# Gated cross-attention block: raw input transposed early, its scale in the rotary table, one GELU pass with a GpSimd copy

## The reference

```
xn  = rmsnorm(layernorm(x)) * (1 + rms_scale)          # per token
q   = rope(xn @ q_w) / 8 ;  k = rope(rmsnorm(mem) @ k_w) ;  v = rmsnorm(mem) @ v_w
x   = x + tanh(g_xattn) * (softmax(mask(q k^T)) v) @ out_w
h   = gelu(layernorm(x) @ ternary(W1)^T + b1)          # 256 -> 1024
x   = x + tanh(g_ffn) * (h @ ternary(W2)^T + b2)       # 1024 -> 256
```

## Time and profile before

| what | value |
|---|---|
| device time, median of 3 runs | 352.86 us (352.55 to 353.22) |
| profiled execution | span 350.0 us from first to last instruction; around it some 2.9 us to the median |
| PE / PEld busy | 313.3 us (90%) / 288.6 us (82%) |
| DVE busy | 276.2 us (79%) |
| ACT busy | 235.6 us (67%) |
| POOL busy | 129.7 us (37%) |
| TensorE clock, mean over the span | 0.961 |
| chain that ended last | PE 42%, DVE 18%, issue 18%, POOL 12%, ACT 6%, DMA 2% |

### The profile page before, as it was taken

How to read it: one execution, slowest core, us unless ns; L and a number is a source line. 1 busy time by engine, 2 the same in 40 slices (tenths; PEclk the granted TensorE clock), 3 DMA queues, 4 the chain that set the end, 5 groups by cost and what they waited for, 6 DMA issues and landing times.

```text
span 350.0 us, 6845 instructions
## 1 busy us (share of the span) xinstructions
PE 313.3 (90%) x2171; PEld 288.6 (82%) x2171; DVE 276.2 (79%) x855; ACT 235.6 (67%) x595; POOL 129.7 (37%) x151
## 2 busy tenths in 40 slices
...
DMA packets 12982, 13.35 MB, mean 38 GB/s; under 512 B 1780, under 2 KB 12396, under 8 KB 12956
## 3 DMA queue, kind: packets, MB, share of 16 engines
...
q0 software_dynamic: 128, 0.21, 0.7%
...
## 4 chain that ended last, share of the span: by engine, by line
PE 42%; DVE 18%; issue 18%; POOL 12%; ACT 6%; DMA 2%; SPq 0%; POOLq 0%; DVEq 0%; ACTq 0%
PE ps_h L919 14%; PE ps_m L919 11%; PE ps_m L1096 6%; DVE xn L647 5%; POOL prob L405 4%; PE ps_t L927 3%; POOL r L367 3%; POOL q_cos L376 3%; PE ps_s L919 3%; DVE pT_lo L652 2%; DMA w_raw<-in_ctx_tail 2%; DVE w_tern L745 1%; ACT prob L527 1%; PE ps_t L1049 1%; DVE vw_lo L728 1%
## 5 line engine op out<-in xcount | busy, mean ns | idle before, releaser
L376 POOL TENSOR_TENSOR q_cos<-q_cos,q_sin 128x256 f32<-128x256 f32 x32 | 25.9, 808 | 133.7 <-DVE q_sin L704 133.7
L919 PE MATMUL ps_h<-x1nT_hi,w_tern 128*128 128x512 f32 x128 | 58.2, 454 | 0.9 <-ACT hT_hi L556 0.9
L1096 PE MATMUL ps_m<-w_tern,hT_hi 128*128 128x256 f32 x224 | 56.8, 292 | 0.1
L919 PE MATMUL ps_h<-x1nT_lo,w_tern 128*128 128x512 f32 x128 | 54.9, 429 | 0.0
L1096 PE MATMUL ps_m<-w_tern,hT_lo 128*128 128x256 f32 x224 | 54.6, 282 | 0.0
L556 ACT ACTIVATE h_all<-ps_h,b_sb 128x512 f32<-128x512 f32 x64 | 44.1, 689 | 13.1 <-PE ps_h L919 11.6
L527 ACT ACTIVATE prob<-s_neg,s_min 128x154 f32<-128x154 f32 x128 | 52.3, 412 | 0.5 <-DVE s_min L765 0.4
L818 DVE TENSOR_TENSOR hT_lo<-h_all,hT_hi 128x512 fp32r<-128x512 f32 x64 | 41.7, 681 | 6.5 <-ACT hT_hi L556 6.5
L919 PE MATMUL ps_m<-vw_hi,pT_hi 128*128 128x256 f32 (+1 forms) x160 | 46.4, 290 | 0.3 <-DVE pT_lo L652 0.3
L405 POOL TENSOR_TENSOR prob<-prob,p_inv 128x512 f32<-128x512 f32 x32 | 33.4, 1043 | 31.8 <-DVE p_inv L769 31.8
L919 PE MATMUL ps_m<-vw_hi,pT_lo 128*128 128x256 f32 (+1 forms) x160 | 44.6, 279 | 0.0
...
## 6 DMA issues: line engine op xcount, KB each, us to landing
...
```

The costliest lines, as they stand in the source:

```text
L376: pool.tensor_tensor(q[:], q[:], q_sin[t % 2][:], ALU.add).then_inc(q_roped, 1)
L919: m = pe.matmul(dst, lhs, rhs, start=(n == 0), stop=(n == len(pairs) - 1))
L1096: m = pe.matmul(dst, a[:, c, P * t:P * (t + 1)], w[:, c, :], start=(c == 0 and a is hT_hi), stop=(c == NF - 1 and a is hT_lo))
```

## The change

Two things change, with what they need around them.

First, `norm1` is gone. TensorE transposes the raw input `x_sb` (`x_T`, tiles `xin0`, `xin1` in `T_ORDER`). The mean is taken out in the weights: in the setup TensorE sums the scaled query weights over the features (a product with ones) and VectorE subtracts the mean (`wq_c`). The factor `r` of each token is multiplied into a copy of the rotary tables on GpSimd (`rope_tables`, one instruction of 128 x 384 into `rq_now`), which `rope` then reads. `x_T` with its hi and lo parts moves from between chunks 3 and 4 to directly behind the fourth `scores`, ahead of `p_T(0)`.

Second, `gelu` runs once per chunk on ScalarE, into `h_act`. GpSimd copies that, rounded, into `hT_hi` (`round_h`, eight per step), and VectorE's `split_h` now waits for GpSimd (`h_hi_set`). Some raw weights lie in room that `prob` lends, with the output weights loaded by four transfers instead of two.

```diff
-        T_ORDER = ("q0", "q1", "q2", "x1n0", "x1n1", "q3", "p0", "tail0", "p1", "tail1", "p2", "tail2",
-                   "xn0", "xn1", "p3", "tail3")
+        T_ORDER = ("q0", "q1", "q2", "x1n0", "x1n1", "q3", "xin0", "xin1", "p0", "tail0", "p1", "tail1", "p2", "tail2",
+                   "p3", "tail3")
...
-            rstd(ve1, r1, ln1_var, ln1_rstd, 0)
-
-            pool.wait_ge(wo_hi_set, 1)
-            pool.tensor_tensor(wo_lo[:], wo_raw[:], wo_hi[:], ALU.subtract).then_inc(wo_set, 1)
+            def rope_tables(i, p):
+                rstd(ve1, r1, ln1_var, ln1_rstd, i)
+                if isinstance(i, int) and i == 0:
+                    pool.wait_ge(rope_in, 32)
+                else:
+                    pool.wait_ge(m_read, m_use(i - 1, f"q{NT - 1}") + 1)
+                pool.wait_ge(ln1_rstd, i + 1)
+                r = r1[:].rearrange("p (t a) -> p t a", a=1).to_broadcast([P, NT, 3 * C // 2])
+                pool.tensor_tensor(rq_now[:], rq_tab[:, NT * p:NT * (p + 1), :], r, ALU.mult).then_inc(rope_scaled, 1)
+
+            rope_tables(0, 0)
+
+            pool.wait_ge(wo_hi_set, 2)
+            for j in range(2):
+                pool.tensor_tensor(wo_lo[:, 2 * j:2 * j + 2], wo_raw[j], wo_hi[:, 2 * j:2 * j + 2],
+                                   ALU.subtract).then_inc(wo_set, 1)
...
+                def round_h(c):
+
+                    if f1:
+                        pool.wait_ge(h_gelu, i * NF + (c + 1 - NF))
+                        pool.sem_inc(h_seen, 1)
+                        pool.tensor_copy(hT_hi[:, c, :], h_act[c % 4][:]).then_inc(h_hi_set, 1)
...
                     w_low_piece(1)
+                round_h(0)
+                round_h(1)
+                normalise(3)
                 if nxt:
-                    rstd(ve1, r1, ln1_var, ln1_rstd, i + 1)
-                normalise(3)
+                    rope_tables(i + 1, 1 - p)
+                for c in range(2, NF):
+                    round_h(c)
...
-                    for dst in (h_act[c % 4][:], hT_hi[:, c, :]):
-                        g = nc.scalar.activation(dst, ps_h[c % 2][:], ACT.Gelu, bias=b1_sb[:, c:c + 1])
-                    g.then_inc(h_gelu, 1)
+                    nc.scalar.activation(h_act[c % 4][:], ps_h[c % 2][:], ACT.Gelu,
+                                         bias=b1_sb[:, c:c + 1]).then_inc(h_gelu, 1)
...
                 exps(2)
+                x_hi()
                 p_hi(0)
...
-                xn_hi()
...
-            dve.wait_ge(wq_scaled, KD)
-            dve.tensor_copy(wq_hi[:], wq_s).then_inc(wq_hi_set, 1)
-            norm1(0, 0)
+            dve.wait_ge(wq_summed, 1)
+            for k in range(KD):
+                dve.scalar_tensor_tensor(wq_c[:, k], ps_h[0][:, 0:H * C], -1.0 / D, wq_s[:, k],
+                                         ALU.mult, ALU.add).then_inc(wq_centred, 1)
+            dve.wait_ge(wq_centred, KD)
+            dve.tensor_copy(wq_hi[:], wq_c).then_inc(wq_hi_set, 1)
...
                 mask_and_min(3)
+                x_lo()
                 p_lo(0)
...
-                    norm1(i + 1, 1 - p)
...
-                xn_lo()
...
-            pe.wait_ge(xn_done, NT)
+            pe.wait_ge(x_in[0], 16)
             for k in range(KD):
-                transposed_tiles(k, ps_t[k], xn, k)
-
+                transposed_tiles(k, ps_t[k], x_sb[0], k)
+
+            pe.wait_ge(wq_scaled, KD)
+            products(ps_h[0][:, 0:H * C], [(ones_sb[:], wq_s[:, k]) for k in range(KD)]).then_inc(wq_summed, 1)
             pe.wait_ge(k_rotated, 2)
...
                 scores(3)
+                x_T()
                 p_T(0)
...
-                xn_T()
```

More of the change, by code:

```diff
@@ L154, in flamingo_block @@
                     for j in range(2))
+        wo_raw = [prob[1 + j][:].rearrange("p h s -> p (h s)")[:, 0:H // 2 * D].rearrange("p (h d) -> p h d", d=D)
+                  for j in range(2)]
+        wkv_raw = prob[3][:].rearrange("p h s -> p (h s)")[:, 0:KD * 3 * C].rearrange("p (k j c) -> p k j c", k=KD, j=3)
         wq_s = prob[0][:].rearrange("p h s -> p (h s)")[:, 0:KD * H * C].rearrange("p (k n) -> p k n", k=KD)
         wq_raw = of_x1.take(KD * H * C).rearrange("p (k n) -> p k n", k=KD)
+        wq_c = wq_raw
         v_tail = of_hi.take(B * H * P).rearrange("p (b h s) -> p b h s", b=B, h=H)
@@ L225, in present @@
             att, nxt, f1, y = has(i)
-            stage = {"q": att, "p": att, "tail": att, "att": att, "xn": nxt, "next_q": nxt, "x1n": f1, "y": y}
+            stage = {"q": att, "p": att, "tail": att, "att": att, "xin": nxt, "next_q": nxt, "x1n": f1, "y": y}
             return [u for u in order if stage[u[:-1]]]
@@ L398, in step @@
                     add_b2()
+                    for c in range(NF):
+                        round_h(c)
                     return
@@ L463, in _ @@
             for r in (0, C):
-                act.dma_start(wo_raw[r:r + C], wo).then_inc(wo_in, 16)
+                for j in range(2):
+                    act.dma_start(wo_raw[j][r:r + C], wo[:, 2 * j:2 * j + 2]).then_inc(wo_in, 16)
             act.wait_ge(gate_in, 16)
@@ L477, in hi_part @@
                 nc.scalar.activation(dst, src, ACT.Copy).then_inc(t_hi, 1)
-            act.wait_ge(wo_in, 32)
-            nc.scalar.activation(wo_hi[:], wo_raw[:], ACT.Copy).then_inc(wo_hi_set, 1)
+            act.wait_ge(wo_in, 64)
+            for j in range(2):
+                nc.scalar.activation(wo_hi[:, 2 * j:2 * j + 2], wo_raw[j], ACT.Copy).then_inc(wo_hi_set, 1)
             for n, (cols, ps) in enumerate(((slice(0, B * P), ps_m[0][:]), (slice(B * P, CT * P), ps_m[1][:, 0:P]))):
@@ L525, in exps @@
                     act.wait_ge(s_masked, i * NT + (t + 1))
+                    if isinstance(i, int) and i == 0 and t == 1:
+                        act.wait_ge(wo_set, 2)
                     for h in range(H):
@@ L641, in variances1 @@
                 variances(i, bn1, mv1, ln1_stats, ve1, ln1_var, 1.0 + RMS_EPS, LN_EPS * RMS_EPS)
-            def norm1(i, p):
-                dve.wait_ge(ln1_rstd, i + 1)
-                for t in range(NT):
-                    dve.tensor_scalar(xn[:, t, :], x_sb[p][:, t, :], mv1[:, t, 0:1], r1[:, t:t + 1],
-                                      ALU.subtract, ALU.mult).then_inc(xn_done, 1)
             def lo_part(n, dst, src, hi):
@@ L973, in vw_product @@
                 if n == 0:
[L974 removed]
+                    pe.wait_ge(wo_set, 2)
                 if n == 2:
```

73 lines of the change are left out of this document (36 added, 37 removed).

## The result

The changed kernel takes 364.5 us (median of 4 runs, 363.6 to 369.3), against 352.7 for the kernel before in the same session (351.9 to 353.2): 1.032 times as long, with an interval of 1.029 to 1.036. A ratio, here and in the experiments, compares undisturbed executions (within 1.5% of the fastest of their kernel; one execution of experiment 9 took 492.8 us), so it need not agree with the quotient of the medians. The forecast was 360.1, in a range of 351 to 367. The profiled execution is the slowest of the four, 369.3 us with a span of 367.5.

The account below looks back on a forecast made before the run. TensorE was taken to bound the steps, with 3.75 us of each given away. Terms +5.0 - 0.5 - 1.2 + 5.1 - 1.2 = +7.2 us on the 350.0 span gave 357.2, plus 2.9 carried over: 360.1 us, range 351 to 367.

Parts of the forecast that it names:

- the 2.9 us that I carried over: Whole kernel: the earlier median of 352.9 us lay 2.9 above its profiled span of 350.0, added to the forecast span.
- Setup, +5.0: Before the steps: VectorE waits for the weight sums, first lo part of the input at 31.2 instead of 26.64 us; +5.0.
- Step 0, -0.5: First step: VectorE binds and loses 2.51 us of norm1, GpSimd's rope_add comes about 1.4 us later; -0.5 us.
- Middle steps, 37.2: Steps 1 to 6: 37.2 us instead of 37.4 at full clock, 0.2 gained six times; -1.2 us.
- The clock, +5.1: TensorE in steps 1 to 6: even chance of half clock after each new hole, three slow stretches of 1.7 us; +5.1.
- Steps 7 to 9, -1.2: Last steps: the second GELU pass no longer holds TensorE twice, 0.6 us each with the restart; -1.2 us.
- The meetings: GpSimd beside VectorE at a step's end: each costs the later one up to about 0.5 us; three on the path.
- Rival (b): TensorE's clock never falls: +1.6 us, 354.5 us in all; chance 0.20.
- Rival (c): GpSimd and VectorE hardly meet: rope_add ends at 214.3, hole 1 us, each step gains 1.2; 348.5 us, chance 0.16.

Follow-up runs that it names:

- experiment 9: Kernel before plus one GELU pass with its copy on GpSimd and add_b2 ahead of the first copy; norm1, late transposes and old setup kept: 356.0 us.
- Experiment 5: Changed kernel with add_b2 ahead of the first copy, and in the setup the key products and key rotation ahead of the wq sums: 349.7 us.
- Experiment 10: Changed kernel with only the raw-input transposes, and their hi and lo parts, back at the old place behind the fourth chunk: 365.8 us.
- experiment 7: Changed kernel with add_b2 ahead of the copies, setup and step 0 reordered, raw-input transposes back at the old place: 335.4 us.
- experiment 12: The kernel of experiment 7 with two GELU passes instead of the GpSimd copies, and add_b2 back ahead of rope_add: 330.8 us.
- experiment 1: Kernel before with only one GELU pass and its rounded copy on GpSimd; norm1 and late transposes kept: 354.6 us.
- experiment 11: Changed kernel with add_b2 as four instructions of 128x256 instead of one of 128x1024, at the same place: 376.8 us.
- experiment 3: Changed kernel with add_b2 moved ahead of the first copy on GpSimd: 354.5 us.
- experiment 4: Changed kernel with the next step's rope_add moved ahead of add_b2 on GpSimd: 365.4 us.

## Why the prediction came out as it did

The direction, the setup and the waits of the middle steps were right. The time was 4.4 us short, and that it was no more is luck: of the +7.2 us of the sum the clock was the largest term and came out at 1.5 instead of 5.1, while step 0, the work of the middle steps and the end were together 9.9 us longer than forecast. By spans, 357.2 was forecast, the profiled execution has 367.5 and the three others have 361.8 to 363.3. Of the 2.9 us that I carried over, 1.8 to 1.9 lie around the span wherever both numbers are known; the rest fits a profiled execution of the kernel before that was 1 us faster than its median. Term by term:

- **Setup, +5.0: right.** The first lo part was forecast at 31.2 us and comes at 30.3 to 32.8 in the five experiments with this setup, against 25.3 to 26.6 with the old one. Experiment 5 gave 3 to 4 of these 5 us back by the order. The clock in the setup, 0 to 1.5 in the forecast, was 4.0 in the profiled execution.
- **Step 0, -0.5: wrong, +4.0.** This is the term that failed. I took VectorE for the bound there and GpSimd as 1.4 us late with 1.08 to spare. The wait at `p_T(0)`, which I had priced for the middle steps only, is 2.07 us in step 0 and goes on through VectorE's `inverse(2)` to `normalise(2)` and to every piece behind it. From there 2.4 us (against the first lo part), the table 0.83, four pieces that meet VectorE 1.45 more than their 6.2, and 0.54 for `rope_add` make 5.2 us; less the 1.08 to spare, 4.1. Experiment 10 shows the cause: with nothing but the transposes back at the old place, `normalise(2)` is 20.3 us behind the first lo part and not 22.4 (20.0 before), the pieces take 1.56 us each, GpSimd has its 1.08 to spare again, and 3.1 of the 4.0 us are gone.
- **Middle steps, 37.2: a size off.** The waits came as forecast: 1.11 for 1.3, 0.37 for 0.3, 1.73 for 2.0. The steps are 37.7 all the same, since TensorE's busy time in a step is 34.5 and not 33.64 us at full clock. Around each hole the busy time grows as well: the first products behind it take longer (a group of transposes 0.66 instead of 0.60), and the last one ahead of it counts in full (0.27 us for a transpose, where the next one otherwise starts after 0.11). I had counted only the idle time. It isn't all of it: experiment 7 has 34.1 us busy with hardly a hole, against 33.6 in experiment 12, and that part stays open.
- **The clock, +5.1: too much, +1.5.** I gave the new hole an even chance of a slow stretch. It fell behind one of the six waits before `q_T(0)` of steps 2 to 7 here, which were of 1.7 to 1.8 us; behind waits of 2.0 to 2.2 us (experiment 1) three times in six, of 2.3 to 2.4 (experiment 10) five in six, of 2.6 to 2.7 (experiment 11) five in six. The even chance would have suited my own figure for the wait, 2.0 us; the wait was 1.73. The three slow stretches that I forecast for steps 1 to 6 are there in number, but two of them lie in step 1, which had one before and is only 0.1 us longer. The clock term was 3.6 too high and step 0 was 4.5 too low, and the two nearly cancel.
- **Steps 7 to 9, -1.2: wrong, +1.0.** The second pass of GELU is gone, but in step 7 the split of the last chunk stands behind `add_b2` as in the middle steps, and TensorE waits 1.93 us for it in step 8. With `add_b2` early (experiment 3) that wait is 0.52.
- **The meetings.** The copy's 0.62 us was right. I priced each meeting at up to 0.5 us, and read the earlier trace rows as speaking against a lock for the whole instruction. The runs are for the lock, in the case of `add_b2`: 2.19 us for a split that meets it late (the changed kernel), 2.77 for one that meets it at its start (experiment 4), 1.24 when it comes in four pieces (11), 0.67 when it isn't there (3). By the Trainium skill (SBUF — State Buffer, section "SBUF: two separate sides") one of the two engines has the ports for the whole instruction and the other blocks; the traces agree for `add_b2`. They agree for `norm1` as well, whose instruction beside `add_b2` takes 2.47 us where its neighbour takes 0.40. That row was in the trace of the kernel before; I had read only the sum of the four, 4.21 us, and it could have told me the price of the split.

  The traces agree for a copy and a split too. These two of the changed kernel meet in the run of four copies:

```profile
221.16 1.07 POOL L415 CAST hT_hi<-h_all 128x512 fp32r<-128x512 f32 x1
...
221.67 1.09 DVE L844 TENSOR_TENSOR hT_lo<-h_all,hT_hi 128x512 fp32r<-128x512 f32 x1
```

  The copy ends at 222.23, 0.48 us after the split ahead of it (which ran to 221.75), and this split at 222.76, 0.53 after the copy. So each waits for the other's end, only the first 0.14 to 0.15 us of an instruction lies outside the lock (0.62 less 0.48, 0.68 less 0.53), and a pair takes 1.01 us. The split of chunk 6 does the same behind `add_b2`, by 0.55. For the ternary pieces the lock doesn't show so: beside a piece that runs from 59.87 to 61.43 the first of VectorE's two instructions in the earlier trace rows runs from 59.91 to 61.09, 1.19 us instead of 0.74, and so ends inside it, and one at 55.81 takes its 0.74 beside another piece. The prediction says that the two ended inside GpSimd's pair; the second ended 0.33 us after it, at 61.76. What I had wrong was to carry that row over to `add_b2`.

Rival (b), the clock that hardly falls, was nearest for the clock. Rival (c) is refuted: in no middle step was `rope_add` ready before TensorE.
